# A recommendation model's forward pass on one core: the order of TensorE's last step, one transposed run split in two, and the filler matmuls removed

## What is computed

```python
x = relu(dense @ Wb0 + bb0)            # 13 -> 512
x = relu(x @ Wb1 + bb1)                # 512 -> 256
d = relu(x @ Wb2 + bb2)                # 256 -> 64
sp = emb[arange(26)[None, :], sparse_idx]          # 26 rows of 64 per sample
T = concatenate([sp, d[:, None, :]], axis=1)       # 27 vectors of 64
Z = einsum('bnd,bmd->bnm', T, T)                   # products of all pairs
h = concatenate([d, Z[:, li, lj]], axis=1)         # 64 + 351
h = relu(h @ Wt0 + bt0)                # 415 -> 512
h = relu(h @ Wt1 + bt1)                # 512 -> 256
p = sigmoid(h @ Wt2 + bt2)             # 256 -> 1
```

## Time and profile before

| | |
|---|---|
| median of 3 executions | 867.12 us (866.83 to 868.22) |
| profiled execution, its own time | 859.53 us |
| its span, first to last instruction | 857.8 us |
| mean granted TensorE clock | 0.62 of full speed |
| PE busy | 319.9 us (37%), 3245 instructions |
| DVE busy | 251.8 us (29%) |
| ACT busy | 18.9 us (2%) |
| POOL busy | 378.5 us (44%) |

### The profile page before, as it was taken

One profiled execution on the slowest core, in us unless ns is written; L12 is line 12 of the kernel. 1 busy time (PEld: TensorE's weight loads), 2 busy tenths in 40 slices (PEclk: granted clock), 3 DMA queues, 4 the chain that ended last, 5 costly groups with the idle time before them and its releaser, 6 DMA issues.

```text
span 857.8 us, 12019 instructions
## 1 busy us (share of the span) xinstructions
PE 319.9 (37%) x3245; PEld 229.5 (27%) x3245; DVE 251.8 (29%) x409; ACT 18.9 (2%) x44; POOL 378.5 (44%) x407
## 2 busy tenths in 40 slices
PE   4627641182014611183013720273113711064815
PEld 1202211181013500171013610162012601053705
DVE  6013442062022532072122532062222621033301
ACT  0000000000000000000000000000000000002201
POOL 6771672526552663616652463706643337700000
PEclk9758785575555855576555855576555855557866
DMA  6330231202321131202321132302311001100000
GB/s 190 28 26 9 25 25 10 21 11 22 21 18 14 20 24 13 24 6 22 24 18 12 17 22 15 28 3 24 25 16 14 14 13 24 27 2 1 3 2 1
DMA packets 20729, 17.87 MB, mean 21 GB/s; under 512 B 11955, under 2 KB 13244, under 8 KB 20665
## 3 DMA queue, kind: packets, MB, share of 16 engines
q0 software_dynamic: 12768, 13.10, 18.2%
q1 hardware_dynamic: 5178, 3.76, 1.5%
q10 hardware_dynamic: 2732, 0.51, 0.3%
HBM read 17.33 MB, written 0.01 MB: 20 GB/s over the span
## 4 chain that ended last, share of the span: by engine, by line
SPq 46%; issue 40%; PE 7%; POOL 3%; DVE 1%; ACT 1%; DMA 0%; another core or an unknown queue 0%; ACTq 0%; DVEq 0%
SPq L391 40%; SPq L338 5%; POOL rows L431 3%; PE ps_gram L549 2%; PE ps_t L683 1%; PE ps_t L662 1%; PE ps_gram L569 1%; PE ps_feat L662 1%; PE ps_feat L596 0%; DVE gram_s L963 0%; PE ps_turn L522 0%; DVE vecs_mv L927 0%; DMA fetched<-in_emb 0%; PE ps_feat L617 0%; PE ps_t L673 0%
## 5 line engine op out<-in xcount | busy, mean ns | idle before, releaser
L431 POOL DMA_INDIRECT rows<-in_emb,idx_row x399 | 376.7, 944 | 370.6 <-issue 367.4
L549 PE MATMUL ps_gram<-vecs_mv,vecs_st 128*32 128x54 f32 x1792 | 69.2, 294 | 183.2 <-issue 158.7
L549 PEld LDWEIGHTS ps_gram<-vecs_mv,vecs_st 128*32 128x32 f32 x1792 | 52.0, 169 | 201.7 <-issue 174.1
L502 PE MATMUL ps_turn<-ident,rows 128*128 128x128 f32 x182 | 33.6, 327 | 183.4 <-DVE rows L921 169.9
L927 DVE COPY vecs_mv<-ps_turn 64x512 f32<-64x512 f32 (+1 forms) x98 | 96.5, 985 | 0.7
L963 DVE STREAM_TRANSPOSE gram_s<-ps_gram 128x864 f32<-128x864 f32 x15 | 16.2, 1083 | 215.9 <-PE ps_gram L549 212.6
L502 PEld LDWEIGHTS ps_turn<-ident,rows 128*128 128x128 f32 x182 | 24.8, 167 | 194.2 <-issue 192.3
L683 PE MATMUL ps_t<-wt_sb,ht_t 128*128 128x256 f32 x128 | 44.4, 496 | 67.4 <-issue 45.2
L927 DVE COPY vecs_st<-ps_turn 128x512 f32<-128x512 f32 (+1 forms) x49 | 47.4, 968 | 16.3 <-remote 9.7
L683 PEld LDWEIGHTS ps_t<-wt_sb,ht_t 128*128 128x128 f32 x128 | 28.6, 240 | 82.7 <-issue 52.7
L921 DVE COPY rows<-fetched 128x128 f32<-128x128 f32 x8 | 1.8, 227 | 146.9 <-DMA fetched<-in_emb 146.9
(11 more groups left out here) (97 smaller groups left out, 270.3 us busy)
## 6 DMA issues: line engine op xcount, KB each, us to landing
fetched<-in_emb ACTq DMA_DIRECT2D x1024, 0.2 KB
fetched<-in_emb SPq DMA_DIRECT2D x1024, 0.2 KB
rows<-in_emb,idx_row POOLq DMA_INDIRECT x399
rows<-in_emb SPq DMA_DIRECT2D x128, 0.2 KB
wt_sb<-in_wt SPq DMA_DIRECT2D x1, 1024.0 KB
wb_sb<-in_wb SPq DMA_DIRECT2D x1, 512.0 KB
wt_early_sb<-in_wt_early SPq DMA_DIRECT2D x1, 512.0 KB
wt_late_sb<-in_wt_late SPq DMA_DIRECT2D x1, 512.0 KB
```

Of the source, the lines that this page charges most:

```text
L431: nc.gpsimd.indirect_dma_start(to, None, emb_rows, bass.IndirectOffsetOnAxis(idx_row[:, c:c + 1], 0)).then_inc(landed, 16)
L502: turned = nc.tensor.transpose(ps_turn[r % 2][:, j, :], rows[:, first + j, :], ident[:, :])
L549: summed = nc.tensor.matmul(ps_gram[32 * v:32 * v + 32, b, g * 2 * VECS:(g + 1) * 2 * VECS], vecs_st[:, c, :], vecs_mv[:, c, :, :].rearran ...
```

## The change

1. `LAST_RUNS` entries get two more fields, `lo, hi`, the transposes of the run. The run (1, 3) becomes two entries, (1, 3, 0, 1) and (1, 3, 1, 2): 12 entries, not 11. The first of the two waits for two gathers on a semaphore of its own (`first_pair_landed`), the second for the other two. `spread_last(11)` is added on ACT and DVE.
2. The two `ps_turn` banks become one tensor, and the late sums go to column block 2 of each of its banks (`late_sums`) instead of `ps_gram`. The wait for `gram_turned` before chunk 0 is gone. The second block of transposed late products moves from `ps_turn[1]` to `ps_gram`.
3. The late chunks are numbered by `gh, b = divmod(l, 2)`; the indices are laid out to match on the host. Chunk 2, half 0 is still the one fetched on SP's queue.
4. PE's order in the last step is new, and all ten `stay_busy` are gone.

```diff
-LAST_RUNS = [(0, r) for r in range(NR)] + [(1, r) for r in range(LATE // 4)]
+LAST_RUNS = [(0, r, 0, 2) for r in range(NR)] + [(1, r, 0, 2) for r in range(HEAD - 1)] + [(1, HEAD - 1, j, j + 1) for j in range(2)]
...
+        ps_turns = ps("ps_turn", [P, 2, 4, P])
+        ps_turn = [ps_turns[:, b] for b in range(2)]
...
-            b, gh = divmod(l, 2)
+            gh, b = divmod(l, 2)
...
+        late_sums = ps_turns[:, :, 2:3, :].rearrange("p b o c -> p b (o c)")
+
+        late_blocks = [ps_feat[1][:, 0, :], ps_gram[:, 0, 0:P]]
...
+                elif (lo, hi) == (0, 1):
+                    pe.wait_ge(first_pair_landed, 32)
                 else:
-                    pe.wait_ge(rows_landed_last[u][r], 64)
+                    pe.wait_ge(rows_landed_last[u][r], 32 * (hi - lo))
...
             def gram_chunk(l):
 
-                if l == 0:
-                    pe.wait_ge(gram_turned, STEPS * 4)
                 wait_spread(LAST_NR + l)
-                b, gh = divmod(l, 2)
+                gh, b = divmod(l, 2)
                 for g in range(4 * gh, 4 * gh + 4):
-                    summed = gram_of(1, b, g, slice(0, SLOTS), slice(EARLY, VECS))
+                    at = 2 * LATE_N * g
+                    for v in range(4):
+                        c = 64 + 16 * v + b * (HALF // 2) + g
+                        summed = nc.tensor.matmul(late_sums[32 * v:32 * v + SLOTS, b, at:at + 2 * LATE_N],
+                                                  vecs_st[:, c, :], vecs_mv[:, c, :, EARLY:VECS], start=True, stop=True)
                 summed.then_inc(late_summed, 1)
...
                 turn_last(9)
-                stay_busy(6)
+                top_1_bias(i, 1)
                 turn_last(10)
-                top_1_bias(i, 1)
+                turn_last(11)
+                gram_early(0)
                 turn_late(0)
-                gram_early()
-                stay_busy(1)
-                turn_late(1)
-                stay_busy(1)
+                gram_early(1)
                 gram_chunk(0)
                 turn_feat_last()
+                turn_late(1)
+                top_0_early(0)
+                top_0_early(1)
                 gram_chunk(1)
                 turn_late(2)
-                top_0_early(0)
-                top_0_early(1)
-                gram_chunk(2)
                 top_0_early(2)
                 turn_late(3)
                 top_0_early(3)
+                gram_chunk(2)
                 gram_chunk(3)
-                stay_busy(1)
                 turn_late_feat()
-                stay_busy(1, ps_gram[:, 1, 0:T1])
                 for m in range(T0 // P):
                     top_0_late(m)
                 top_1_sum(i, 1)
```

More of the change, by code:

```diff
@@ L215, in build @@
         probs = sb("probs", [P, 2 * STEPS])
-        ps_turn = [ps(f"ps_turn{b}", [P, 4, P]) for b in range(2)]
+        ps_turns = ps("ps_turn", [P, 2, 4, P])
+        ps_turn = [ps_turns[:, b] for b in range(2)]
         ps_gram = ps("ps_gram", [P, 2, 512])
@@ L237, in build @@
         late_landed = [sem(f"late_landed{n}") for n in range(CHUNKED)]
+        first_pair_landed = sem("first_pair_landed")
         pair_base_ready = sem("pair_base_ready")
@@ L310, in turned_last @@
         def turned_last(k, h):
-            u, r = LAST_RUNS[k]
+            u, r, lo, hi = LAST_RUNS[k]
             part = slice(DIM * h, DIM * (h + 1))
@@ L317, in turned_last @@
             else:
-                places = [(slice(64 * u, 64 * (u + 1)), slice(4 * r, 4 * r + 4),
-                           ps_turn[k % 2][part, 0:2, :].rearrange("p j (t c) -> p (j t) c", t=2))]
+                places = [(slice(64 * u, 64 * (u + 1)), slice(4 * r + 2 * lo, 4 * r + 2 * hi),
+                           ps_turn[k % 2][part, lo:hi, :].rearrange("p j (t c) -> p (j t) c", t=2))]
             for cs, ts, source in places:
@@ L349, in early_products @@
             return ps_gram[:, :, 0:HALF * EARLY].rearrange("p b (c v) -> p v b c", v=EARLY)[:, 0:n]
-        late_blocks = [ps_feat[1][:, 0, :], ps_turn[1][:, 0, :]]
+        late_sums = ps_turns[:, :, 2:3, :].rearrange("p b o c -> p b (o c)")
+        late_blocks = [ps_feat[1][:, 0, :], ps_gram[:, 0, 0:P]]
         def unrolled_early():
@@ L440, in gather_pairs @@
                     for h in range(2):
-                        gather(LAST_COLS + 4 * j + 2 * u + h, half(2 * j + u, h), rows_landed_last[u][r])
+                        first = (u, j) == (1, 2 * (HEAD - 1))
+                        gather(LAST_COLS + 4 * j + 2 * u + h, half(2 * j + u, h),
+                               first_pair_landed if first else rows_landed_last[u][r])
             for i in range(STEPS - 1):
@@ L515, in turn_last @@
                     pe.wait_ge(fetched_moved, STEPS)
+                elif (lo, hi) == (0, 1):
+                    pe.wait_ge(first_pair_landed, 32)
                 else:
-                    pe.wait_ge(rows_landed_last[u][r], 64)
+                    pe.wait_ge(rows_landed_last[u][r], 32 * (hi - lo))
                 if k >= 2:
                     wait_spread(k - 2)
-                for j in range(2):
+                for j in range(lo, hi):
                     slot = FETCHED - 1 + j if r == NR - 1 else 4 * r + 2 * j + u
@@ L572, in gram_of, with gram_early @@
                 return summed
[L574 to L581, removed]
+            def gram_early(b):
+                if b == 0:
+                    pe.wait_ge(gram_turned, (STEPS - 1) * 4 + 2)
+                    wait_spread(LAST_NR - 1)
+                for g in range(HALF // 2):
+                    summed = gram_of(1, b, g, slice(0, EARLY), slice(0, EARLY))
+                if b == 1:
+                    summed.then_inc(gram_summed, 1)
             def gram_chunk(l):
-                if l == 0:
-                    pe.wait_ge(gram_turned, STEPS * 4)
                 wait_spread(LAST_NR + l)
-                b, gh = divmod(l, 2)
+                gh, b = divmod(l, 2)
                 for g in range(4 * gh, 4 * gh + 4):
-                    summed = gram_of(1, b, g, slice(0, SLOTS), slice(EARLY, VECS))
+                    at = 2 * LATE_N * g
[3 more added lines that the diff above has]
+                                                  vecs_st[:, c, :], vecs_mv[:, c, :, EARLY:VECS], start=True, stop=True)
                 summed.then_inc(late_summed, 1)
@@ L829, in last_step @@
                 spread_last(10)
+                spread_last(11)
                 spread_late(0)
@@ L944, in stand_late @@
                 dve.wait_ge(late_summed, CHUNKED)
-                products = ps_gram[:, :, 0:HALF * LATE_N].rearrange("p b (c v) -> p v b c", v=LATE_N)
+                products = late_sums.rearrange("p b (c v) -> p v b c", v=LATE_N)
                 nc.vector.transpose(late_s[:, :, :].rearrange("p k c -> p (k c)"), products).then_inc(late_stood, 1)
@@ L1151 @@
     pair_idx = last[:, 0:FETCHED - 1].reshape(2, 64, 2 * PAIRED_RUNS, 2, 2).transpose(3, 1, 2, 0, 4).reshape(P, -1)
-    late_idx = last[64:, LATE:LATE + LATE_N].reshape(4, 2, 2, 4, LATE_N, 2).transpose(4, 0, 3, 1, 2, 5).reshape(P, -1)
+    late_idx = last[64:, LATE:LATE + LATE_N].reshape(4, 2, 2, 4, LATE_N, 2).transpose(4, 0, 3, 2, 1, 5).reshape(P, -1)
     fetch_idx = idx[:, :, FETCHED, :].reshape(PARTS, PART, STEPS, 2).transpose(3, 0, 2, 1).reshape(2 * PARTS, STEPS * PART)
```

## The result

The changed kernel takes 865.12 us (median of 22 executions, 862.32 to 867.16), the kernel before 867.19 us in the same comparison (22 executions, 863.85 to 873.7). The two medians differ by 2.07 us. The ratio is 0.9969, with a 95% interval of 0.9958 to 0.998: 2.7 us less, between 1.7 and 3.6. The forecast was 1.4 us less, 865.7.

What follows compares the result with a forecast made beforehand. SP's last landing plus a tail of PE work was taken to bound the kernel. PE's `top_0_late` would start 2.65 us earlier, the clock hand back 1.2: 1.45 us less in span, median 867.12 - 1.4 = 865.7, range 864.5 to 867.9.

Steps and rivals of the forecast that it cites:

- rival 1: Last step's tail: the clock stays at 1.2 GHz to the end; gain 0.35 us, time 866.8; chance 0.18.
- rival 2: Tail: the clock rises early, by the end of `top_0_late`; gain 2.0 us, 865.1 (at 850: 2.6, 864.5); chance 0.17.
- rival 4: Last step: nothing changes, as PE doesn't wait for the landing or the reordered work is hidden; 867.1 us; chance 0.05.
- the case that was chosen: Tail: the clock rises at about 852.5, inside `top_1_sum`; 1.45 us less in span, 865.7 us; chance 0.50.
- SP's last landing sets the end: End of kernel: PE idles 24.47 us for SP's last fetches, then a tail of PE work follows.
- Head parts worth nothing under cover: Ahead of the landing: split run, extra spread, early order and eight removed fillers gain 0 on the path.
- The early blocks moved ahead: `top_0_early(0)` and `(1)` go from behind the landing transpose into PE's idle time: gain 1.71 us.
- The two fillers behind the landing: Removing those behind `gram_chunk(3)` and `turn_late_feat`: gains of 0.35 us (0.2 to 0.6) and 0.25 us (0 to 0.5).
- `top_0_late` 2.65 us earlier: Tail: with all reordering and filler gains `top_0_late` starts at 847.9, not 850.53; bounds 1.9 to 3.3 us.
- The clock hands 1.2 us back: `top_0_late` and `top_1_sum`: more work falls before the clock's rise at 852.5, giving back 1.2 of 2.65 us.
- The rule against the change: All PE work: keep TensorE continuously busy; by it, dropping the ten fillers would make the tail miss the clock's rise.
- Rival 3: Tail: ordinary executions of before rise early thanks to fillers, the changed one stays low; slower, 867.9 to 869; chance 0.10.

Runs made afterwards that it cites:

- first experiment: The kernel before without its two fillers behind the landing: 869.37 us against 869.70, ratio 0.9998.
- second: The kernel before with only `top_0_early(0)` and `(1)` moved ahead of `turn_late(2)`: 867.85 us against 869.70, ratio 0.9977.
- third experiment: The kernel before with the new PE order and no fillers, but no split run and late sums in `ps_gram`: 867.64 us against 869.70, ratio 0.9988.
- twelfth: The changed kernel once more, no edit, the second comparison with the kernel before: 867.41 us (12 executions) against 866.95, ratio 1.0001.
- fourth: The changed kernel with the two fillers behind the landing put back: 867.38 us against 869.70 for before, ratio 0.9983.
- fifth run: The kernel before with all of late chunk 2 gathered by POOL, SP's last 128 fetches gone: 834.49 us against 858.98, ratio 0.9705.
- sixth run: The changed kernel with all of late chunk 2 gathered by POOL: 839.24 us, ratio 0.9755 to before.
- ninth: The changed kernel with late chunk 2 gathered by POOL and ten fillers put back: 843.87 us against 866.95 for before, ratio 0.9732.
- tenth: The kernel before with late chunk 2 gathered by POOL and no fillers: 843.17 us, ratio 0.9724 to before.
- seventh run: The changed kernel with every row gathered by POOL, no row-by-row fetch on SP and ACT: 780.78 us, ratio 0.9091 to before.

## Why the prediction was right

The range (864.5 to 867.9) and the place held, and in the first comparison the direction too. The size was forecast at 1.4 us and measured at 2.7 (1.7 to 3.6) there, and at nothing (1.8 less to 2.1 more) in the second, of fewer executions; the forecast lies just outside the first interval and inside the second. The range was wide enough to hold rivals 1, 2 and 4 as well, so a time within it doesn't prove the case that was chosen. The seven profiled tails say more (all in us behind the landing transpose):

| run | order | fillers behind the landing | DVE's late transpose | first matmul of `top_0_late` | rise | end of `top_1_sum` |
|---|---|---|---|---|---|---|
| before | old | yes | 5.56 | 7.72 | 9.9 | 12.45 |
| first | old | no | 5.56 | 7.12 | 10.1 | 12.33 |
| second | old, two blocks moved | yes | 4.70 | 6.86 | 7.0 | 10.60 |
| changed kernel | new | no | 3.42 | 4.98 | 8.1 | 10.27 |
| third | new | no | 3.42 | 4.98 | 10.2 | 11.29 |
| twelfth | new | no | 3.42 | 4.98 | 9.5 | 10.91 |
| fourth | new | yes | 3.41 | 5.57 | 5.7 | 9.33 |

The new order without fillers ended at 10.8 on average, the old at 12.4. That is 1.6 us, near the 1.45 of the sum. Some of that nearness is luck, since single tails of the same instructions differ by 1.0 us with the moment of the rise. The case that was chosen, a low level as `top_1_sum` begins, came in the third and twelfth runs; in the changed kernel's first profile rival 2 came (2.18 us shorter, 865.12 us, against its 2.0 and 865.1). Why one comparison shows 2.7 us and the other nothing stays open: the profiled executions differ by up to 14.7 us ahead of the landing, so a difference of a microsecond there can't be followed in one profile each.

Point by point, by its own steps:

- *SP's last landing sets the end.* Right: PE started 1.03 and 1.11 us after SP's last issue, and the fifth run removed the landing and 24.5 us with it.
- *Head parts worth nothing under cover.* Right: the third experiment, without split run or new place for the sums, has the same distances. But PE took longer ahead of the wait, not less: from SP's last fetch of the 26th table to the start of the idle stretch 31.0 us (796.83 to 827.78) against 27.4 (790.73 to 818.13), and the idle stretch shrank from 24.47 to 21.02 us. Without the cover the head isn't free (sixth run).
- *The early blocks moved ahead: 1.71, "the surest term".* Mis-assigned. Alone it is 0.86, since the moved piece had covered a spread (0.78 us of new wait). The chunk gram's new place behind `top_0_early(3)`, priced at 0.35, frees the rest, 1.28 by the difference of the second and third runs (4.70 - 3.42). The sum of the two terms was 2.06 and measured 5.56 - 3.42 = 2.14.
- *The two fillers behind the landing: 0.35 + 0.25.* Measured 0.60 in one direction (first experiment) and 0.59 in the other (fourth).
- *`top_0_late` 2.65 us earlier.* 2.74, counted by the first matmul (7.72 to 4.98).
- *The clock hands 1.2 us back.* This is the mis-sized term: it was sized by one moment, 9.9 us behind the landing, and in this order the rise came at 8.1, 10.2 and 9.5. What was handed back, against before's one profiled tail, was 0.56, 1.6 and 1.2 us (2.74 less the shortening of 2.18, 1.16 and 1.54). One of its bounds was also read too simply: the lag of 3.8 us was counted from 800.9, but the level was still 1.00 then and fell only in 801 to 804, so it was no rise out of a low stretch of that length.
- *The rule against the change.* The Trainium skill (*TensorE: Matmul & The Clock Gate*, section "Why this matters for your kernels") asks for continuous work. Its full consequence, rival 1, came in none of the profiled tails: the level always rose before the end. By degree the tails lean towards the rule, without showing it. Counted from the start of `top_0_late`, the rise came 3.0, 3.2, 4.5 and 5.3 us later in the four tails with PE gaps and no fillers, and 2.2, 0.1 and 0.1 us later in the three with fillers. But fillers also delay `top_0_late`, and counted from the landing the two groups overlap: 8.1 to 10.2 without, 5.7, 7.0 and 9.9 with. Elsewhere the level was lost for 17 us without fillers (sixth run), and for 3.4 us with ten of them (ninth).
- *Rival 3 (slower).* No tail of the changed order stayed low to its end. Its other half, that ordinary executions of before rise early, was not tested: before was profiled once in the tail, with a late rise. The second comparison, with no gain, leaves room for it.

## What to carry to other kernels

Find the event that the last stage waits for, and count only what stands behind it: everything ahead of it was free here, and the same edits cost 4.7 us by the medians (intervals overlapping) once that event was gone. Moving work out from behind a wait gains only what it didn't itself cover; look at which other wait it was hiding, and move the waiter too. And look at the cover before polishing under it: 128 row fetches on one queue took 48.6 us where one gather of 0.94 us on an idle engine did the same, and replacing all of them won 80 us where the change won 2.7 us in one comparison and nothing in the other. And before a profile is used to explain a time, look where its execution lies among the timed ones: the sixth run's profile is its slowest execution, the tenth's its fastest.

## What the runs showed of the hardware

- 128 direct DMAs of 256 bytes on SP's queue took 48.58 and 48.61 us with their address loads, 0.38 us each, though no other queue was issuing (before: POOL's last gather at 748.89, ACT's last fetch ended at 760.6); the gather of the same 128 rows is one POOL instruction of 0.94 us, 1.25 us apart from the next.
- PE's idle time in front of the grams with no visible releaser did not go with the fetches: 158.7 us before, 159.9 us with none of them on SP and ACT (seventh run). I had expected the two to be one. What causes it stays open.
- TensorE's level rose between 5.7 and 10.2 us after work began again behind the landing, in seven tails that differ by little; in before's it rose only after 9.9 us in which PE had no gap. Three executions of the same instructions behind the landing ended at 10.27, 10.91 and 11.29 us.
- The level also fell without a long gap: in the ninth run at 826.0, with no PE gap over 1.2 us in the 10 us before.
